# Sorting tokens on chip with a 0/1 matrix on TensorE in a fused mixer and two-expert layer

## The reference

```
mod = (silu(c) @ wmod).reshape(4, 6, 1, 512)          # shift/scale/gate rows sa, ca, ga, sb, cb, gb per sequence
ga, gb = sign(g) * max(|g|, 0.25)                      # both gates are clamped
h = layernorm(x) * (1 + ca) + sa                       # first modulation
x = x + ga * mixer(h)
h = layernorm(x) * (1 + cb) + sb                       # second modulation
x = x + gb * experts(h)

mixer(h):   xc = causal depthwise conv, 4 taps (h)
            B, C, d = h @ Wxproj.T ; delta = softplus(d)
            state scan over the 512 tokens: s = exp(A*delta)*s + delta*B*(xc @ Winproj.T)
            return (C*s) @ Woutproj.T + D*xc
experts(h): each token goes to one of 2 experts (larger router logit), weighted by its softmax
            a = leaky(h @ w_fc.T, 0.5)**2 ; return weight * (a @ w_proj.T)      # hidden size 2048
```

## Time and profile before

| what | value |
| --- | --- |
| times of three runs, us | 613.67, 616.06, 618.61 |
| span of the profiled execution, first to last instruction, us | 626.6 |
| its mean granted TensorE clock | 0.936 of full |
| busy share of the span: PE, DVE, ACT, POOL | 87%, 63%, 45%, 33% |

### The profile page before, as it was taken

How to read it: one execution, slowest core, us unless ns; L and a number is a source line. 1 busy time by engine, 2 the same in 40 slices (tenths; PEclk the granted TensorE clock), 3 DMA queues, 4 the chain that set the end, 5 groups by cost and what they waited for, 6 DMA issues and landing times.

```text
span 626.6 us, 11028 instructions
## 1 busy us (share of the span) xinstructions
PE 545.7 (87%) x3052; PEld 441.0 (70%) x3052; DVE 394.7 (63%) x801; ACT 282.3 (45%) x679; POOL 209.2 (33%) x185
## 2 busy tenths in 40 slices
PE   5989959494528899999999999999999999998860
PEld 0435444453327899999999999999999999987750
DVE  3697889898893565454555545555545455567862
ACT  2668583532114455454445445455445445432320
POOL 1030276684886121122122122122112212157541
PEclk9999969789658999999999999999999999999996
DMA  8911543030267520201201202202101010077641
GB/s 314 390 69 52 217 152 120 0 137 1 84 235 236 222 69 2 70 16 51 69 0 67 67 0 67 67 0 67 64 3 67 6 61 0 0 242 245 182 143 67
DMA packets 17042, 61.40 MB, mean 98 GB/s; under 512 B 3051, under 2 KB 3051, under 8 KB 13688
## 3 DMA queue, kind: packets, MB, share of 16 engines
q1 hardware_dynamic: 11256, 42.63, 19.3%
q0 software_dynamic: 5760, 18.43, 8.2%
HBM read 47.30 MB, written 14.27 MB: 98 GB/s over the span
## 4 chain that ended last, share of the span: by engine, by line
PE 71%; DVE 11%; issue 8%; ACT 3%; DMA 2%; another core or an unknown queue 2%; POOL 1%; DVEq 0%; SPq 0%; ACTq 0%; POOLq 0%
PE bank L912 32%; PE bank L940 28%; PE bank L756 3%; DVE xc L1076 3%; PE bank L821 2%; DVE junk L1151 1%; PE bank L774 1%; PE bank L789 1%; PE bank L826 1%; DVE u L1089 1%; DMA sorted_tokens<-gap,gapI 1%; DVE st L1019 1%; DMA wm<-wmod 1%; DVE res L1126 1%
## 5 line engine op out<-in xcount | busy, mean ns | idle before, releaser
L490 POOL TENSOR_TENSOR Wlo<-raw,Whi (+1 forms) x64 | 82.3, 1290 | 276.4 <-ACT Whi L651 276.3
L912 PE MATMUL bank<-XShi,Whi 128*128 (+1 forms) x576 | 165.7, 288 | 5.7 <-DVE twice_h L1341 4.9
L912 PE MATMUL bank<-XShi,Wlo 128*128 (+1 forms) x576 | 164.1, 285 | 0.0
L912 PE MATMUL bank<-XSlo,Whi 128*128 (+1 forms) x576 | 164.1, 285 | 0.0
L1360 DVE TENSOR_TENSOR acc<-acc,bank 128x512 f32 (+1 forms) x126 | 85.9, 687 | 71.7 <-PE bank L940 66.6
L1341 DVE TENSOR_TENSOR twice_h<-relu_h,bank 128x256 f32<-128x256 f32 x144 | 60.2, 420 | 99.4 <-ACT relu_h L713 96.8
L912 PEld LDWEIGHTS bank<-XShi,Whi 128*128 128x128 f32 x576 | 111.6, 194 | 12.1 <-issue 9.8
L940 PE MATMUL bank<-Whi,ahi 128*128 128x512 f32 x272 | 107.9, 397 | 6.6 <-DVE alo L1349 6.5
L912 PEld LDWEIGHTS bank<-XSlo,Whi 128*128 128x128 f32 x576 | 111.6, 194 | 2.1
L912 PEld LDWEIGHTS bank<-XShi,Wlo 128*128 128x128 f32 x576 | 111.5, 194 | 0.0
L940 PE MATMUL bank<-Wlo,ahi 128*128 128x512 f32 x272 | 107.3, 394 | 0.0
(11 more groups left out here) (146 smaller groups left out, 605.9 us busy)
## 6 DMA issues: line engine op xcount, KB each, us to landing
raw<-wffn SPq DMA_DIRECT2D x16, 1024.0 KB, 5.2
wm<-wmod SPq DMA_DIRECT2D x6, 1024.0 KB, 12.4
res_row<-sorted_residuals SPq DMA_DIRECT2D x18, 260.0 KB
sorted_rows<-sorted_tokens SPq DMA_DIRECT2D x9, 512.0 KB, 10.8
x_in<-x SPq DMA_DIRECT2D x4, 1024.0 KB, 10.1
bc<-mod_rows SPq DMA_DIRECT2D x4, 772.0 KB, 7.0
ga_bc<-ga_rows SPq DMA_DIRECT2D x4, 256.0 KB, 3.5
wx_sb<-wx SPq DMA_DIRECT2D x1, 514.0 KB, 10.7
```

What stands on the lines that cost most here:

```text
L490: pool.tensor_tensor(Wlo[:, hb % 2, c, :], raw[:, c, :], Whi[:, hb % 2, c, :].bitcast(F32), ALU.subtract).then_inc(s_wlo, 1)
L912: mm = pe.matmul(hP[m][:, 0:TILE], W[wp][:, par, 2 * e + k // 2, o:o + P], XS[xp][:, k, bass.ds(t * TILE, TILE)], start=(n == 0), stop=(n ...
```

## The change

The sorted h2 rows are no longer written to DRAM and read back. ACT writes the normalized rows (`z2`, not yet modulated); DVE makes for each block of 128 tokens a 0/1 matrix `perm` from the ranks in the block; PE multiplies the block by it (`permuted_block`), which transposes and sorts it at once; ACT evicts the four feature blocks with the second modulation as per-partition scale and bias to a running offset of `XSfull` (`place`), once counted from the front, and the same 128 columns are copied to where they lie counted from the back. Sequence by sequence the tokens that belong elsewhere are overwritten by the next block. The residual rows still go by indirect DMA.

With it go many other edits: PE has two output banks (`pO`) where it had four, and interleaves the permuted blocks of b - 1 with the outputs of b; the skip products of a sequence are issued later; the first layernorm's statistics move from ACT to DVE (`stats1`); the router's products are taken from `res` and not from the normalized rows, so that only one row for each sequence is broadcast; `ranks` and `permutations` follow the third tap of the convolution; the tiny rank instructions no longer lie inside `scan`; POOL clears `XSfull` once (9216 elements in each partition); the early weight splits are 4 + 4, in b = 2 and 3, where they were 3 + 3 + 2. Where `XSfull` is [partition, row, k], its feature blocks have a stride of 4 elements.

```diff
@@ POOL
-                for n, j in enumerate(h2_by_pool(b)):
-                    pool.wait_ge(s_lg, TJ * b + j + 1)
-                    pool.tensor_tensor(h2[:, j, :], h2[:, j, :], bc[:, b, 0:DM], ALU.mult).then_inc(s_h2m, 1)
...
-                for j in range(TJ):
...
-                    pool.indirect_dma_start(out=rows_dram, out_offset=bass.IndirectOffsetOnAxis(ap=posI[:, b % 2, j:j + 1], axis=0),
-                                            in_=h2[:, j, :], in_offset=None).then_inc(s_sc1, 16)
...
+            pool.wait_ge(s_mr, 7)
+            pool.wait_ge(s_mc, 3)
+            pool.wait_ge(s_md, 64)
+            pool.memset(XSfull[:, :, :], 0.0).then_inc(s_fill, 1)
@@ ACT
+            def place(b):
+                act.wait_ge(s_off, b + 1)
+                first = [act.value_load(offI[0:1, b % 2, j:j + 1], min_val=0, max_val=P * (TJ * b + j)) for j in range(TJ)]
...
+                for j in range(TJ):
+                    n = TJ * b + j
+                    act.wait_ge(s_pz, n + 1)
+                    wait(act, s_e1, n)
+                    for k in range(KT):
+                        act.activation(XSfull[:, bass.ds(first[j], P), k], pT[j % 2][:, P * k:P * k + P], ACT.Identity,
+                                       bias=cols[:, 4, k, b:b + 1], scale=cols[:, 3, k, b:b + 1]).then_inc(s_e0, 1)
+                    if b < NB - 1:
+                        act.wait_ge(s_e0, KT * (n + 1))
+                        act.activation(XSfull[:, bass.ds(first[j] + (FROM_BACK - P * n), P), :],
+                                       XSfull[:, bass.ds(first[j], P), :], ACT.Copy).then_inc(s_e1, 1)
...
             for b in range(NB):
+                if b + 1 < NB:
+                    exp_minus_abs(b + 1)
+                    log_part(b + 1)
+                if b == 1:
+                    guess1(3)
+                guess2(b)
+                normalize2(b)
+                if b == 1:
+                    normalize1(3)
+                if b + 1 < NB:
+                    decay(b + 1)
+                    diagonals(b + 1)
+                margin_exp(b)
                 if b + 2 < NB:
+                    modulate1(b + 2)
                 for c in EARLY.get(b, ()):
                     act.wait_ge(s_raw[c // 4], 16)
                     split(0, c)
...
+                place(b)
@@ PE
             def skip_product(b, j):
+                wait(pe, s_x2, TJ * b + j - 1)
...
+            def permuted_block(b, j):
+                n = TJ * b + j
+                if j < 2:
+                    pe.wait_ge(s_hT, KT * min(b + 3, NB))
+                wait(pe, s_e0, KT * (n - 1))
+                pe.wait_ge(s_pm, n + 1)
+                pe.wait_ge(s_z2, n + 1)
+                for k in range(KT):
+                    mm = pe.matmul(pT[j % 2][:, P * k:P * k + P], z2[:, j, P * k:P * k + P], perm[:, j, :], start=True, stop=True)
+                mm.then_inc(s_pz, 1)
...
             for b in range(NB):
+                nxt = b + 1 < NB
+                if b > 0:
+                    permuted_block(b - 1, 0)
+                    permuted_block(b - 1, 1)
+                pe.wait_ge(s_hm, b + 1)
+                pe.wait_ge(s_wg, b + 1)
+                state_output(b, 0)
+                state_output(b, 1)
+                for j in (2, 3):
+                    if b > 0:
+                        permuted_block(b - 1, j)
+                    skip_product(b, j)
+                    state_output(b, j)
+                if nxt:
                     delta_product(b + 1)
                 if b == 0:
+                    mod_row(3)
                     mod_row(4)
+                if nxt:
+                    B_C_products(b + 1)
+                if b == 0:
+                    pe.wait_ge(s_mr, 5)
+                    pe.wait_ge(s_bu, 1)
+                    mod_columns((3, 4))
                     mod_row(5)
...
+                if b + 2 < NB:
+                    transposes1(b + 2)
+                prefix(b)
+                if nxt:
...
                     state_product(b + 1)
...
+                    skip_product(b + 1, 0)
+                    skip_product(b + 1, 1)
@@ DVE
                 if nxt:
...
+                    softplus_residue(b + 1)
+                if b == 0:
+                    own.link(mod_row(3, modrow[0:NB, 3, :], 1.0))
+                    dve.tensor_tensor_reduce(wdrow[:, :], modrow[0:NB, 3, :], wdiff[:, :], 1.0, 0.0, ALU.mult, ALU.add,
+                                             scrow[:, 1:2]).then_inc(s_mr, 1)
+                if b == 1:
+                    stats1(3)
+                stats2(b)
+                if nxt:
                     softplus(b + 1)
...
+                    own.link(mod_row(4, modrow[0:NB, 4, :], 0.0))
...
                 newton2(b)
                 if b == 0:
...
+                    columns(3, 5, 3).then_inc(s_cols, 1)
+                if b == 1:
+                    newton1(3)
+                margin_products(b)
+                margins(b)
+                candidates(b)
+                if b == 0:
+                    mod_row(5, modrow[0:NB, 5, :], 0.0).then_inc(s_mr, 1)
+                    dve.wait_ge(s_mr, 6)
+                    clamp_row(5)
+                if nxt:
+                    conv(b + 1, 2, range(KT), taps)
+                ranks(b)
+                permutations(b)
...
+                positions(b)
+                top_weight(b)
...
+            for j in range(TJ):
+                n = TJ * b + j
+                dve.wait_ge(s_e0, KT * (n + 1))
+                dve.wait_ge(s_e1, n)
+                dve.tensor_copy(XSfull[:, bass.ds(first[j] + (FROM_BACK - P * n), P), :],
+                                XSfull[:, bass.ds(first[j], P), :]).then_inc(s_e1, 1)
@@ SP
-            sp.dma_start(mod_dram, packed[:, :]).then_inc(s_md, 16)
...
+            sp.dma_start(wd_dram, wdrow[:, :]).then_inc(s_md, 16)
+            sp.dma_start(sc_dram, scrow[:, :]).then_inc(s_md, 16)
...
-            load_rows(range(FIRST))
...
-            load_rows(range(FIRST, NT))
```

More of the change, by code:

```diff
@@ L164, in build @@
[L164 to L171 removed]
+        diag = take("diag", [P, 2, KT, P])
+        wx_sb = take("wx_sb", [P, KT, 2 * S + 1])
+        win_sb = take("win_sb", [P, KT, S])
+        woutg = [take(f"woutg{b}", [P, DM]) for b in range(2)]
+        cur[0], limit[0] = o_a, o_const
@@ new lines, in build @@
+        woutg += [take(f"woutg{b}", [P, DM]) for b in range(2, NB)]
+        wout_sb = take("wout_sb", [P, DM])
+        wdb = take("wdb", [P, KT, P])
+        perm = take("perm", [P, TJ, P])
+        wm = [at(f"wm{n}", [P, KT, 512], F32, o) for n, o in enumerate((o_raw, o_raw + ZB, o_whi, o_whi + ZB, o_wlo, o_wlo + ZB))]
+        cur[0], limit[0] = o_acc, o_a
+        ga_bc = take("ga_bc", [P, NB, DM])
+        modrow = take("modrow", [NB, 6, DM])
+        wdrow = take("wdrow", [NB, DM])
+        scrow = take("scrow", [NB, SC])
@@ L246, in build @@
         s_gbc = sem("ga_broadcast_landed")
-        s_bc = [sem(f"mod_broadcast_landed{b}") for b in range(NB)]
+        s_bc = sem("router_rows_landed")
         s_md = sem("mod_stored")
@@ L766, in mod_columns, with transposes1 @@
                 mm.then_inc(s_mc, 1)
-            def transposes1(b, ks=range(KT)):
-                for k in ks:
+            def transposes1(b):
+                for k in range(KT):
+                    if k < 2 and b >= 2:
+                        wait(pe, s_e0, KT * TJ * (b - 2))
                     wait(pe, s_hT, KT * b + k - 1)
@@ L899, in _ @@
+            for j in range(TJ):
+                permuted_block(NB - 1, j)
             PARTS = ((0, 0), (0, 1), (1, 0))
@@ L1237, in _ @@
             columns(0, 2, 1).then_inc(s_cols, 1)
-            own.link(mod_row(2, modrow[0:NB, 2, :], 0.0))
-            clamp_row(2)
             dve.wait_ge(s_A, 1)
             dve.tensor_scalar(Acol[:, :], Acol[:, :], -1.0, None, ALU.mult).then_inc(s_An, 1)
+            stats1(1)
             taps = {}
@@ L1246, in _ @@
             softplus(0)
+            newton1(1)
             conv(0, 2, range(KT), taps)
+            own.link(mod_row(2, modrow[0:NB, 2, :], 0.0))
+            dve.wait_ge(s_cols, 1)
+            clamp_row(2)
             columns(2, 3, 2).then_inc(s_cols, 1)
```

569 lines of the change are left out of this document (195 added, 374 removed).

## The result

| | before | changed |
|---|---|---|
| median of four runs each, us | 617.19 (613.67 to 618.61) | 638.14 (635.95 to 640.03) |
| ratio, 95% interval | | 1.0353 [1.0307, 1.0399] |
| span of the profiled execution, us | 626.6 | 634.2 |
| first `fc` of hidden block 1, us | 248.60 | 268.86 |
| from block 7's first `fc` to the end of the span, us | 80.5 | 67.9 |

What follows compares the result with a forecast made beforehand. DVE was taken to bound the mixer phase before. Last mask at 196.9, plus 17.5 and 49.6, starts block 1 at 264.0 against 248.6, 15.4 us later; 616.06 + 15.4 = 631.5, said as 632 us, range 617 to 647.

Steps and rivals of the forecast that it cites:

- The case is decided in the mixer phase: Before the experts: removing the DRAM trip gains only some 1.3 us, so mixer gains and losses decide; last mask at 196.9.
- the two banks and the late taps: Mixer phase: output products wait for residuals, third taps stand behind margins; with the broadcast, the forecast's slowdown, chance 0.60.
- hm(3): Milestone on DVE: state of sequence 3 ready for the output products; 162.9 us before, forecast 180.8, 17.9 later.
- To the next hm: Mixer period from third tap to next state ready: 12.6 us in b = 1, 7.5 in b = 2, state product slowed.
- The direct part: From last mask to expert start: 17.5 us with perm, serial evictions and copies, XShi/XSlo and POOL's hold, against 18.8 before.
- I leave block 0 at 49.6: First expert hidden block: loses 16 PE transposes, gains a cold start, so its length is kept at 49.6 us.
- Removing the DRAM trip gains some 1.3 us: From last mask to expert start: 17.5 us against 18.8, serial evictions taking the trip's place.
- What the mixer phase gains: POOL's 28 h2 instructions go: DVE saves 7.7 us in the margins and 3.5 at 101 us, likewise next period.
- Strides: Rival: the 16-byte step in `XSfull` doubles instructions, +10, 642 us; +4 if only the stream doubles; chance 0.13.
- Full clock and quick broadcast: Rival: PE keeps full clock, `woutg` and broadcast at their low ends; loss falls to 4 to 5, 620 us; chance 0.16.
- DVE alone: Rival: PE and ACT run ahead, periods are DVE's work, 31.7 and 27.7 us; kernel about 601 us; chance 0.11.
- The clearing of `XSfull`: POOL's clearing, 9.3 us from about 88 on: costs 0 to 6 us by its hold on DVE, taken as 0.

Runs made afterwards that it cites:

- e10: Changed kernel with four output banks again and the placing of b - 1 behind the delta product (PE) and exp_minus_abs (ACT); ratio to before 1.035.
- e11: Changed kernel with third taps ahead of the margins in periods 0 and 1, PE's state product earlier in period 1, `XSfull` cleared in four parts; ratio to before 1.034.
- e1: Changed kernel with evictions of placed blocks and XShi/XSlo reads at a step of one element instead of four (result wrong); ratio to before 1.035.
- e14: e13 with ACT's decay and diagonals ahead of normalize2, the last guess earlier, and block 0's XShi/XSlo of tile t + 2 later; ratio to before 0.983.
- e12: Changed kernel with e10, e11 and the last sequence's blocks from the back evicted by DVE straight from PSUM, all together; ratio to before 1.003.
- e13: e12 with further reordering: modulate1(2), mod_row(3), state product and period 2's third taps earlier, last placings and weight splits changed; ratio to before 0.999.
- e7: Kernel before with sorted rows read from x, so loads do not wait for the scatters, which are still issued (result wrong); ratio to before 0.999.
- e8: Kernel before without POOL's 28 h2 modulation instructions, so the experts get unmodulated rows (result wrong); ratio to before 0.976.
- e3: Changed kernel with third taps ahead of the margins (DVE), state product ahead of prefix (PE) and modulate1 earlier (ACT); ratio to before 1.044.

## Why the prediction came out

The forecast was 632, the measurement 638.1; the sign held, the time lay in the range, and the two waits that it named are there. But two of its parts were off in opposite directions, -6.6 and +11.5, so that the time came out near is partly luck. "The case is decided in the mixer phase" is only half true: I had 16.7 us of loss up to the last mask and a gain of 1.3 behind it, and the traces have 10.1 and 10.2 us of loss. What the sum took for its causes, the two banks and the late taps, e10 and e11 bear out only in part: 3.6 and 3.5 us at hm(3) when undone singly.

**The mixer phase was over-priced by 6.6 us** (last mask forecast at 196.9, measured 190.3). Most of its terms held: from hm(1) to the residue 13.5 against 14.7, from there to the end of the third taps 16.9 against 16.5, period 0 55.7 against 56.4. Of the 6.6 us, 2.9 are in period 1, 1.7 in period 2, and 0.6 to 0.7 each in hm(0), period 0 and the stretch from hm(3) to the mask. The largest mis-sized term is PE's clock in "To the next hm": I took the state product at 5.8 and twice 6.0, and the PE timeline shows 4.52, 4.36 and 5.52 us, 3.4 us less in all. At full clock eight such instructions take 3.60, so the state product begins at half clock, as I had said, and full clock comes back within it (granted 0.79 from 93 to 98 us, 0.63 from 165 to 172, 1.00 from 172 to 183). The skips and permuted blocks behind it take 1.95 for 16, at full clock:

```profile
134.66 4.36 PE L722 MATMUL bank<-xc,win_sb 128*128 128x512 f32 x8
138.86 1.95 PE L736 MATMUL bank<-diag,xc 128*128 128x128 f32 x16
140.64 1.95 PE L758 MATMUL bank<-perm,z 128*128 128x128 f32 x16
...
166.48 5.52 PE L722 MATMUL bank<-xc,win_sb 128*128 128x512 f32 x8 [0.24 <-DVE xc L959]
```

In before an idle stretch of 8.16 us was followed by four tiny matmuls, eight transposes and the skips, all at half clock:

```profile
121.22 1.95 PE L774 MATMUL bank<-ident,z 128*128 128x128 f32 x8
```

Here the idle stretches are 9.82, 8.17 and 5.33 us in periods 0, 1 and 2, and eight, 16 and no transposes stand between them and the state product. No run isolates this, so the reason for the earlier return stays open.

**The direct part was under-priced by 11.5 us.** From mask to block 1 I had 17.5 + 49.6 = 67.1; it is 23.2 + 55.4 = 78.6. The first eviction comes 4.8 after the mask, as summed. The four links take about 2.5 each instead of 2.0 and the hold 4.9 instead of 3: 14.9 against 10.8. XShi and XSlo take 3.5 against 1.9. Those are mis-sized terms. "I leave block 0 at 49.6" is a step that failed: I counted only instructions on PE, while in the tiles of block 0 ACT and DVE have nearly as much to do as PE has (from 240 to 257 us PE is busy for 14.6, DVE for 14.5, ACT for 13.0), and an XSlo of 2.1 us for a pair placed ahead of `alo` is exposed. e1 and e14 give it: 3.0 of the 5.8 go with the strides, and with the strides left in the other order gives back 3.7 (from e12) to 4.7 (from e13). These two overlap; the cold start is in both, with 2.2 us in the first `fc` alone.

**"Removing the DRAM trip gains some 1.3 us"** sets a start counted back from block 1, 199.0, against a real first `fc` with a steady block behind it. The real first `fc` was at 188.5, with a block 0 of 60.1 us. The changed kernel's block 0 is 4.7 shorter, but it starts 25.0 later. e7 shows no gain without the trip, within 3.5 us, but does not settle its price, as said there.

**"What the mixer phase gains"**: 7.7 in the margins was less than half of it; e8 has 18.1 up to the mask for the h2 work. The 3.5 at 101 us do not belong to it: in e8, where `low` stays, that instruction still takes 4.54. In the changed kernel they are gone all the same (0.69), because no `low` runs before 176 us.

**The rivals.** *Strides*: a real price in XShi and XSlo, 4.5 us in all, close to the "+4" that its own counter-argument gave; of its larger terms, the last evictions have 0.5 us instead of 5, and the placing does not outlast the delta product (the wait before `softplus_residue` is 4.03 us in period 0 too, which has no placing). *Full clock and quick broadcast*: neither half came as stated. The clock came back early but not ahead of the state products, which gave 3.4 us, and the margins began at 79.8 (forecast 79.2). *DVE alone*: its periods of 31.7 and 27.7 are not reached even by e14 (36.3 and 30.7), where DVE in both still waits for ACT, 0.84 us before `softplus_residue` and 2.10 and 1.21 before `newton2`.

**The clearing of `XSfull`** was left at 0 and is nearly off the path in the changed kernel: `perm` is stretched from 0.87 to 2.72, but the product of DVE that needs PE's state product starts at 98.2, and without the clearing it would have waited for that product until 97.9. In e3 one `den` of four elements took 7.36 us beside it. The Trainium skill (SBUF — State Buffer, Who interferes with whom) says that copies and scalar forms can contend with GpSimd, and two-input forms only with a GpSimd instruction that reads; the traces agree, with these two scalar forms held and four taps, of which the last runs beside the clearing, at 2.72. The clearing takes 7.78 us, 0.84 ns for each element, where I had scaled 9.3.

## What to carry to other kernels

Price a moved instruction by who stands behind it on its engine: other orders of the same pieces, with a few more banks, brought block 1 29.8 us forward. When one removed wait changes little, take it away together with the wait that takes its place before calling it free: three edits worth 11.5 singly gave 16.9 together. And measure a start by a real instruction, not by counting back from a steady stage.

## What the runs showed of the hardware

A read of 128x512 float32 at a step of 16 bytes takes 1.11 instead of 0.62 us on ACT and 1.09 instead of 0.69 on DVE; four ACT writes of 128 columns at that step take 1.62 instead of 1.50. The Trainium skill (SBUF — State Buffer, Door 1: The DMA port swizzle) names a penalty for each access that crosses to a new 16-byte line; these rows agree. A DVE TENSOR_SCALAR that reads PSUM and writes SBUF was not held by `low` (1.47 for four), an SBUF to SBUF copy was, 5.33 for 0.43. Stalls in which ACT waits for nothing that the trace shows appear in the last block (up to 4.6 us in before, 7.3 in e12) and at the start of block 0 (3.61 in e7). The DMA engines are busy there (share 0.77 in before from 566 to 586 us), but the changed kernel has 0.66 and 0.83 in its last block without such stalls, so busy DMA engines alone do not bring them. Medians of one kernel lay 1.6% apart between chips.
